# Layer 1 of a four-layer cross-attention kernel: waits of the probability turns, order of the first two batches

## The reference

```python
h = concat([x, latents])                       # 256 keys and values
q = latents @ q_w + q_b ;  k, v = h @ kv_w + kv_b
attn = softmax(where(mask, q @ k.T / 32, -inf))  # 16 heads, 128 x 256
attn_out = (attn @ v) @ out_w + out_b + residual
out = rmsnorm(attn_out, postnorm_w)
out = gelu(out @ mlp_w1 + mlp_b1) @ mlp_w2 + mlp_b2 + residual
```

## Time and profile before

| | us |
|---|---|
| time, median of 3 runs | 2207.16 |
| the three runs | 2203.24, 2207.16, 2207.83 |
| the profiled execution, its own time | 2207.91 |
| its span | 2206.1 |
| PE busy | 2109.5 (96%) |
| DVE busy | 1179.2 (53%) |
| ACT busy | 1098.7 (50%) |

### The profile page before, as it was taken

One profiled execution on the slowest core, in us unless ns is written; L12 is line 12 of the kernel. 1 busy time (PEld: TensorE's weight loads), 2 busy tenths in 40 slices (PEclk: granted clock), 3 DMA queues, 4 the chain that ended last, 5 costly groups with the idle time before them and its releaser, 6 DMA issues. The chain is left out here.

```text
span 2206.1 us, 56005 instructions
## 1 busy us (share of the span) xinstructions
PE 2109.5 (96%) x21728; PEld 1525.5 (69%) x21728; DVE 1179.2 (53%) x3275; ACT 1098.7 (50%) x3372; POOL 558.8 (25%) x573
## 2 busy tenths in 40 slices
PE   8997799999999999999778999999999999999987
PEld 4445477777777777776566877877787787777764
DVE  4774333333333333333345666666776666777654
ACT  4564344444444444444123565555566555556634
POOL 0001000000000000000144444444444444444420
PEclk9999899999999999999879999999999999999988
DMA  5531433333333333333350222222221222222121
GB/s 167 186 134 60 108 102 100 99 97 96 96 96 101 102 103 98 101 98 84 106 146 7 52 52 51 56 66 62 56 56 50 51 57 61 66 56 54 49 55 35
DMA packets 211422, 180.57 MB, mean 82 GB/s; under 512 B 92960, under 2 KB 171168, under 8 KB 208928
## 3 DMA queue, kind: packets, MB, share of 16 engines
q1 hardware_dynamic: 202080, 152.74, 27.0%
q0 software_dynamic: 2240, 12.58, 1.7%
q10 hardware_dynamic: 6912, 12.59, 1.5%
HBM read 96.04 MB, written 46.14 MB: 64 GB/s over the span
## 5 line engine op out<-in xcount | busy, mean ns | idle before, releaser
L791 PEld LDWEIGHTS bank<-normedT,mlp_w 128*128 128x128 f32 x2048 | 233.3, 193 | 11.1 <-issue 9.9
L791 PE MATMUL bank<-normedT,mlp_w 128*128 128x128 f32 x2048 | 239.2, 278 | 0.8 <-DVE normedT L1050 0.8
L801 PE MATMUL bank<-mlp_w,geluT 128*128 128x512 f32 x512 | 224.7, 592 | 0.0
L2175 ACT ACTIVATE scores_turned<-scores_turned,nmax 128x128 f32<-128x128 f32 x480 | 185.4, 391 | 20.8 <-DVE nmax L2425 20.8
L801 PEld LDWEIGHTS bank<-mlp_w,geluT 128*128 128x128 f32 x512 | 95.0, 190 | 108.1 <-issue 108.1
L1652 POOL TENSOR_TENSOR k_even_odd<-k_even_odd,decay_products 128x512 f32<-128x512 f32 x80 | 94.7, 1184 | 280.0 <-PE quad L1850 137.1
L1001 DVE CUSTOM_DVE_ANT_0 probs<-quad,neg_mask 128x256 f32<-128x256 f32 x256 | 90.8, 421 | 109.3 <-PE quad L746 109.3
L2325 DVE COPY_PREDICATED wkv_scores<-level_masks,quad 128x1024 f32<-128x1024 int32 x64 | 99.1, 1549 | 72.6 <-PE quad L1855 43.4
L912 ACT ACTIVATE probs<-probs,nmax 128x256 f32<-128x256 f32 x256 | 126.6, 496 | 12.2 <-DVE nmax L1001 11.7
L2425 DVE CUSTOM_DVE_ANT_0 scores_turned<-quad,mask 128x128 f32<-128x128 f32 x480 | 104.1, 286 | 42.3 <-PE quad L1969 42.1
L650 POOL COPY latents_b<-latents_b_next 128x512 f32<-128x512 f32 x16 | 9.8, 610 | 449.3 <-DVE l_x L1059 410.5
(11 more groups left out here) (267 smaller groups left out, 4358.9 us busy)
## 6 DMA issues: line engine op xcount, KB each, us to landing
l_blocks<-probs_turned_blocks SPq DMA_DIRECT2D x128, 256.0 KB, 2.7
probsT<-l_blocks SPq DMA_DIRECT2D x256, 128.0 KB, 3.5
probsT<-scores_turned SPq DMA_DIRECT2D x240, 64.0 KB, 2.0
scores_turned<-scores_turned SPq DMA_DIRECT2D x240, 64.0 KB
mlp_w<-in_mlp_w POOLq DMA_DIRECT2D x8, 1024.0 KB, 5.6
x_in<-l_out SPq DMA_DIRECT2D x32, 256.0 KB, 3.8
x_in<-in_x SPq DMA_DIRECT2D x16, 256.0 KB, 2.6
ctx_in<-in_ctx SPq DMA_DIRECT2D x16, 256.0 KB, 2.9
```

What stands on the lines that cost most here:

```text
L791: mm = nc.tensor.matmul(ps[:, f * P:(f + 1) * P], mlp_w1[:, c, m * P:(m + 1) * P], nT[:, c, :], start=(c == 0), stop=(c == NC - 1))
L801: mm = nc.tensor.matmul(PS[u.bank][:, :], gT[:, f, :], mlp_w2[:, f, :], start=(f == 0), stop=(f == NF - 1))
L2175: ac = nc.scalar.activation(s, s, ACT.Exp, bias=nmax[:, k, 2 * c + e:2 * c + e + 1], scale=-1.0, accum_out=rsum[:, kv, gr:gr + 1])
```

## The change

Three edits, all in layer 1.

The turn of piece m waits for the store of piece m of the half ahead, not for the loads of that half. In batch 0 DVE takes maxima, normalisation and turn of the first half before it takes those of the second. In batch 1 PE computes scores(1, half 0) ahead of attend(0), and ACT's copies of both key halves go ahead of squares(0), for which batch 1 is written out in front of ACT's loop.

```diff
@@ PE, batch(i, first)
                     if first:
                         keys(i, 0)
                         keys(i, 1)
+                        scores(i, 0)
                     attend(i - 1)
...
                     values(i, 1)
-                    scores(i, 0)
+                    if not first:
+                        scores(i, 0)
                     hidden(i - 1, 0)
@@ ACT
-                def batch(i, last=False):
+                def batch(i, first=False, last=False):
                     copy_q(i)
                     copy_k(i, 0)
+                    if first:
+                        copy_k(i, 1)
                     squares(i - 1)
-                    copy_k(i, 1)
+                    if not first:
+                        copy_k(i, 1)
...
-                with act.Fori(1, B - 1) as i:
+                batch(1, first=True)
+                with act.Fori(2, B - 1) as i:
                     batch(i)
@@ DVE, turn_probs(i, half)
                     n = 2 * i + half
-                    if not isinstance(n, int) or n > 0:
-                        dve.wait_ge(s_probsT, MOVES * n)
                     dve.wait_ge(s_norm, HH // 2 * (n + 1))
...
                     for m in range(NB):
+                        if not isinstance(n, int) or n > 0:
+                            dve.wait_ge(s_blocks[m], 16 * n)
+                            dve.sem_inc(s_hold, 1)
                         nc.vector.transpose(turned[:, :, m, :, :], blocks[:, :, m, :, :]).then_inc(s_turned, 1)
@@ DVE, batch 0
-                for g in range(NG):
-                    maxima(0, g)
-                probabilities(0)
+                for half in range(2):
+                    for g in range(4):
+                        maxima(0, 4 * half + g)
+                    normalise(0, half)
+                    turn_probs(0, half)
```

## The result

The changed kernel takes 2196.48 us (median of 7 runs, 2191.69 to 2202.54) against 2207.16 us before (7 runs, 2201.40 to 2209.75). The ratio is 0.9957, with a 95% interval of 0.9938 to 0.9976: 5 to 14 us faster, 10.7 by the medians. The profiled execution took 2196.48 us, its span is 2194.7 us.

The account below looks back on a forecast made before the run. PE was taken to bound the loop, busy 756.00 of 756.00 us, waiting only at its two ends. Gains of 4.05 + 1.1 + 2.16 + 3.1 = 10.4 us gave 2197 us, range 2193 to 2203.

Parts of the forecast that it names:

- the forecast case: Whole kernel: faster by 10.4 us, to 2197 us, with the clock staying up over project(15); chance 0.53.
- The idle time ahead of the turns is worth nothing in the loop: Loop of layer 1: DVE's 46.0 us idle ahead of the turns gains nothing, since PE is always busy there.
- Part 1: Front, batch 0: second turn at 224.24, attend(0)'s second half at 235.42 in place of 239.47; gain 4.05 us.
- Part 2: Front: scores(1, 0) run inside PE's wait for attend(0) and vanish from PE's busy part; gain 1.1 us.
- Part 3: End: the last half's turn starts 2.16 us earlier, shortening the wait for attend(15)'s second half; gain 2.2 us.
- 0.4 us for stores behind loads: End: early stores stand behind the first half's loads in ring order; at most 0.4 us shared, 2.16 becoming 1.8.
- Part 4: End: the clock stays up for project(15), 3.60 us in place of 6.74; gain 3.1 us (0 to 3.1).
- the clock falls again: End: wait ahead of project(15) is shorter, not gone, so the clock drops; gain 7.3, 2200.6 us; chance 0.25.
- The clock at the front: Front: clock stays at half for attend's second half and most of project(0), the wait still some 7 us; no gain.
- its last rival: Both ends: end trip shrinks to 11.18 us and front clock recovers sooner, up to 1.5 us; 2195 us; chance 0.08.
- the half clock behind the wait for turn_normed(15): End: the 2.97 us wait ahead of turn_normed stays, and so does the half clock behind it; no gain.
- overlapping stores and loads slow the loop: Loop: trips 3 to 4 us longer make PE wait, paid 14 times; for example 2212.3 us; chance 0.04.

Follow-up runs that it names:

- second profile: The changed kernel, unaltered, compared and profiled once more against the kernel before: ratio 0.9946 (0.9931 to 0.9961).
- values early and filled: Changed kernel with values(1, 0) ahead of attend(0), values(1, 1) ahead of turn_normed(0), and unread extra matmuls in PE's waits at both ends: ratio 0.9921 to the kernel before.
- filled closer: As values early and filled, with six extra matmuls, not five, between attend(0)'s halves and one ahead of project(0) and project(15): ratio 0.9905, 2187.72 us.

## Why the prediction was right

The predicted 2197 lies 0.5 us from the measured median, and the forecast case, faster by its 10.4 us, is the one that came. The mechanism held: nothing in the loop, all of the gain at its two ends. That the sum came so close is partly luck, as the points show:

- *The idle time ahead of the turns is worth nothing in the loop.* Shown by the run with the new wait in batch 0 only.
- *Part 1, 4.05 us at the front.* Measured 4.07, and 4.10 in the second profile. The steps hold as well: the second turn of batch 0 started 19.34 us behind the scores; predicted were 19.36 (224.24 less 204.88). SP was free of the first half's loads 0.7 us later than worked out, still ahead of the next store. What I had not seen is that this gain does not need the order of batch 0: with the old order the new wait gives 3.6 us by itself. The turn was only the nearest of two holds; behind it stand SP's issue and the full DMA engines.
- *Part 2, 1.1 us.* Measured 1.16 inside the changed kernel. Alone it gave nothing measurable.
- *Part 3, 2.16 us at the end, was too large.* Measured 1.70 and 1.41. Two of its numbers were off. The hand-over ahead of the turn is 0.34 us and not 0.15. And the trip from the turn to attend took 12.44 us (1032.55 to 1044.99) against 12.15. Over the five profiles with the new wait there and nothing filled in it took 12.39 to 12.79, over the four with the old one 11.71 to 12.15: 0.7 us longer in the mean. The prediction's 0.4 us for stores behind loads does not show as the cause: in both kernels the DMA engines take up the second half's data about 1.9 us behind its turn. Why the trip is longer stays open. With the old wait PE waited 3.04 to 3.45 us there over four profiles, with the new one 1.73 to 2.14 over five: about 1.3 us is what the edit is worth.
- *Part 4, 3.1 us of clock.* In the profile 3.08, so it reads as right; over the runs it is too large. Without extra matmuls project(15) took 6.74, 6.62, 5.19 and 5.18 us with the old wait, and 3.67, 3.67, 3.67, 5.93 and 5.18 with the new one: 5.9 against 4.4 in the mean, so 1.5 us. The rival "the clock falls again" is what happens in two of five; that the forecast's case came in the profile compared is luck in part.
- *The clock at the front, costed at nothing, was worth 1.4 us.* Without extra matmuls project(0) took 5.08 to 5.15 us in the four profiles with all of the front's edits, and 6.11 to 6.54 in all those without. The prediction had this only in its last rival, at up to 1.5. A second term that it had at nothing, the half clock behind the wait for turn_normed(15), gave 1.30 in the profile.
- *How the sum came out.* The four parts gave 10.0 us in the profile, these two terms and the loop 2.8 more, and layers 0, 2 and 3 took 1.5 back. Over the other profiles the two terms largely make up for parts 3 and 4, which were too large. A sum of which several terms are off by one to two microseconds met the median within 0.5 us by luck.
- *The rival that overlapping stores and loads slow the loop* did not come about: no PE wait arose in the loop. The overlap itself is real where the old order of batch 0 makes it large, and there it costs about 1 us.

## What to carry to other kernels

Idle time ahead of an instruction is a prize only where the bounding engine waits behind it; here 29 of 44 us of it could come back and the time of the loop did not move by 0.1 us. A software pipeline with a full loop is tuned at its two ends: besides shortening the first wait (4.1 us here), look for work of the next batch that can stand in it (scores 1.2 us, values 2.4). And count a TensorE wait twice: once for itself, and once for the half clock that may follow; two gaps of under 1 us close together were followed by one here.

## What was not expected of the hardware

The granted clock fell to half behind two gaps of 0.89 and 0.95 us with 1.08 us of small attention matmuls between them, though PE had been fully busy for 8 us ahead; with the second gap filled it did not. At the end of layer 1, gaps of 1.75 and 0.95 us left it up. The Trainium skill ("TensorE: Matmul & The Clock Gate", Part 1) has activity releasing a clock that is throttled by default; the direction agrees, and these gaps are shorter than I took to matter.

Layers 2 and 3, which no run touched, took 1107.5 us in the profile before, 1107.7 after, 1103.0 in the run with values early and filled, and 1111.6 in the one filled closer. That is nearly as wide as the spread between runs of one kernel, and is the reason why the places in the traces tell more here than the times. The windows of these layers, in the run with values early and filled and in the one filled closer, show what differs:

```profile
1080.78:2183.80 1103.02, 1057.86 (x15356) 818.42 (x15356) 723.63 (x2084) 584.26 (x2061) 469.49 (x470) 0.98 0.24 57
1079.68:2191.30 1111.62, 1065.27 (x15356) 822.99 (x15356) 723.51 (x2084) 584.99 (x2061) 469.35 (x470) 0.97 0.24 57
```

The same 15356 matmul records kept PE busy 7.4 us longer, at a granted clock of 0.97 in place of 0.98; PE's idle time differs by only 1.2 us. So most of the spread in these layers comes with the clock. What moves the clock from execution to execution stays open.
